# A lightning-attention block on one core: last gates ahead of the norm's root, first rows normalised by halves, two transfers moved

## The reference

```python
xn = layernorm(x)                          # x: 2048 tokens x 512, fp32
s = lightning_attn(xn, slopes, w_qkv, w_gate, w_out, norm_w)
g = silu(ffn(xn, router_w, router_b, expert_b))
x = x + s * g

# lightning_attn: 16 heads of 128, 2 sequences of 1024 tokens, blocks of 64
qkv = silu(xn @ w_qkv.T)
# per head: causal linear attention with decay exp(-slope * distance), by a state kv
out = norm_w * (out * rsqrt(mean(out * out) + 1e-6))   # mean over all 2048 values of a token
y = (sigmoid(xn @ w_gate.T) * out) @ w_out.T
# ffn: softmax over 64 router scores, the 8 largest kept;
#      flat * sum(weights) + weights @ expert_bias
```

## Time and profile before

| | us |
|---|---|
| median of 3 runs (1069.09 to 1071.27) | 1070.4 |
| the profiled execution | 1068.64 |
| its span, first to last instruction | 1066.8 |
| TensorE busy | 1047.1 (98%) |
| VectorE / ScalarE / GpSimd busy | 750.0 / 515.5 / 634.2 |

### The profile page before, as it was taken

One profiled execution on the slowest core, in us unless ns is written; L12 is line 12 of the kernel. 1 busy time (PEld: TensorE's weight loads), 2 busy tenths in 40 slices (PEclk: granted clock), 3 DMA queues, 4 the chain that ended last, 5 costly groups with the idle time before them and its releaser, 6 DMA issues.

```text
span 1066.8 us, 15997 instructions
## 1 busy us (share of the span) xinstructions
PE 1047.1 (98%) x5626; PEld 895.0 (84%) x5626; DVE 750.0 (70%) x1286; ACT 515.5 (48%) x807; POOL 634.2 (59%) x513
## 2 busy tenths in 40 slices
PE   6999999999999999999999999999999999999997
PEld 5888888888888888888878888888888888888886
DVE  6847657676765778768667766766776776876866
ACT  5746363553536335453554535435453543535344
POOL 3737475665747547474756957657474745747435
PEclk9999999999999999999999999999999999999999
DMA  7273524435252432526757264342525335242442
GB/s 243 80 276 93 140 66 130 107 99 119 58 136 65 129 89 67 140 66 172 257 191 177 94 151 129 109 110 72 135 69 130 90 104 112 51 127 82 131 127 80
DMA packets 259920, 128.12 MB, mean 120 GB/s; under 512 B 223360, under 2 KB 223488, under 8 KB 259840
## 3 DMA queue, kind: packets, MB, share of 16 engines
q1 hardware_dynamic: 259840, 127.09, 43.6%
HBM read 86.95 MB, written 40.11 MB: 119 GB/s over the span
## 4 chain that ended last, share of the span: by engine, by line
PE 92%; DVE 2%; DMA 1%; issue 1%; POOL 1%; ACT 1%; SPq 0%; POOLq 0%; DVEq 0%
PE st_ps L544 18%; PE st_ps L546 17%; PE st_ps L545 17%; PE score_ps L666 5%; PE out_ps L719 5%; PE out_ps L721 5%; PE out_ps L720 5%; PE head_ps L702 5%; PE tk_ps L685 4%; PE head_ps L705 4%; PE st_ps L532 1%; PE st_ps L534 1%; PE st_ps L533 1%; DMA xt_lo<-spill_lo 1%; POOL acc L1567 1%
## 5 line engine op out<-in xcount | busy, mean ns | idle before, releaser
L544 PE MATMUL st_ps<-xt_hi,w_hi 128*128 128x512 f32 x826 | 336.9, 408 | 1.4 <-DMA xt_lo<-spill_lo 1.3
L546 PE MATMUL st_ps<-xt_hi,w_lo 128*128 128x512 f32 x826 | 323.2, 391 | 0.0
L545 PE MATMUL st_ps<-xt_lo,w_hi 128*128 128x512 f32 x826 | 322.1, 390 | 0.0
L546 PEld LDWEIGHTS st_ps<-xt_hi,w_lo 128*128 128x128 f32 x826 | 155.0, 188 | 34.7
L1456 POOL TENSOR_TENSOR w_lo<-land_a,w_hi 128x1024 fp32r<-128x1024 f32 x44 | 107.0, 2433 | 128.7 <-ACT w_hi L1048 128.7
L544 PEld LDWEIGHTS st_ps<-xt_hi,w_hi 128*128 128x128 f32 x826 | 155.6, 188 | 31.1 <-issue 2.1
L545 PEld LDWEIGHTS st_ps<-xt_lo,w_hi 128*128 128x128 f32 x826 | 155.7, 189 | 27.9
L1436 POOL TENSOR_TENSOR w_lo<-land_a,w_hi 128x768 fp32r<-128x768 f32 x44 | 83.9, 1906 | 147.9 <-ACT w_hi L1043 147.9
L719 PE MATMUL out_ps<-wo_hi,gate_hi 128*128 128x512 f32 x240 | 96.3, 401 | 0.6 <-DVE acc L1772 0.5
L1774 DVE TENSOR_TENSOR acc<-acc,out_ps 128x512 f32<-128x512 f32 x104 | 71.3, 685 | 32.5 <-PE out_ps L721 32.2
L721 PE MATMUL out_ps<-wo_hi,gate_lo 128*128 128x512 f32 x240 | 93.8, 391 | 0.0
(11 more groups left out here) (330 smaller groups left out, 2072.9 us busy)
## 6 DMA issues: line engine op xcount, KB each, us to landing
land_a<-wgrp_dram SPq DMA_DIRECT2D x48, 512.0 KB, 3.7
v_row<-v_squares SPq DMA_DIRECT2D x120, 128.0 KB, 3.2
k_row<-k_squares SPq DMA_DIRECT2D x120, 96.0 KB, 2.9
v_squares<-v_t SPq DMA_DIRECT2D x45, 256.0 KB, 2.7
land_b<-wo_dram SPq DMA_DIRECT2D x16, 512.0 KB, 4.5
land_b<-wgrp_dram SPq DMA_DIRECT2D x14, 512.0 KB, 4.2
k_squares<-state SPq DMA_DIRECT2D x15, 384.0 KB, 2.3
k_squares<-v_t SPq DMA_DIRECT2D x15, 384.0 KB, 4.7
```

Of the source, the lines that this page charges most:

```text
L544: pe.matmul(ps[:, :], w_h2, x_h2, start=first and k == 0, stop=False, skip_group_check=True)
L545: pe.matmul(ps[:, :], w_h2, x_l2, start=False, stop=False, skip_group_check=True)
L546: end = pe.matmul(ps[:, :], w_l2, x_h2, start=False, stop=last and k == 1, skip_group_check=True)
```

## The change

The statistics of the first four tiles are combined one by one behind each tile's own. The first four tiles are normalised by halves of 256 columns: tiles 0 to 2 by VectorE, tile 3 by ScalarE, and fills 0, 1 and 2, 3 wait for their half. VectorE takes fills (0, 8) and (0, 9) before it normalises the rows of `bp` 1, and on all three engines `turn_and_score(0, 0)` (with its followers) goes ahead of `fill(1, 0)`. `swap_keys` is cut in `keys_out` and `keys_back`, and in step 7 the load of B21 goes between the two. In the tail bias products 4 to 7 and quarters 2 and 3 of the last gate block go ahead of the sums of squares; the last two squares are added on GpSimd and VectorE, not by TensorE, so a sum has one matmul call for each tile; the last gates are split on VectorE ahead of the root; tile 0's old sum goes into the output bank by a product with the identity, and its x is added by join_last; the last tile is joined and stored in halves.

```diff
@@ declarations
-        tail_square = k_t[:, 0, :]
+        tail_square = st_ps[2][:, :]
@@ SP
-            def swap_keys(ss, h):
+            def keys_out(ss, h):
...
                 sp.dma_start(k_squares, src[:, 0:2 * (NCH - 1) * HD]).then_inc(k_out, 16)
-                sp.wait_ge(k_out, 16 * (at + 1))
+
+            def keys_back(ss, h):
+                sp.wait_ge(k_out, 16 * (2 * (ss - 1) + h + 1))
                 sp.wait_ge(kv_full, unit(ss, h, 0))
...
-                swap_keys(ss, 1)
+                keys_out(ss, 1)
+                if ss == PAIRS - 1:
+                    renew_block(B21, P2)
+                keys_back(ss, 1)
...
-                if ss == PAIRS - 1:
-                    renew_block(B21, P2)
                 load_group(after, ss + 1, VAL)
...
-            for t in range(TILES):
+            for t in range(TILES - 1):
                 sp.wait_ge(summed_v, t + 1)
                 sp.dma_start(out_t[2 + t // NCH][:, t % NCH, :], acc[:, t // NCH, t % NCH, :]).then_inc(stored1, 16)
+            for i in range(2):
+                half = slice(i * (HID // 2), (i + 1) * (HID // 2))
+                sp.wait_ge(summed_v, TILES + i)
+                sp.dma_start(out_t[3][:, NCH - 1, half], acc[:, 1, NCH - 1, half]).then_inc(stored1, 16)
@@ PE, rows_there: fills 0 and 1 wait for the left halves, fills 2 and 3 for the right
+                if bp == 0 and b == 0 and c < 3:
+                    pe.wait_ge(ln_row, 3 * half + c + 1)
+                elif bp == 0 and b == 0:
+                    pe.wait_ge(ln_row_a, half + 1)
...
@@ PE, sum_squares loses the second matmul; output_rows of tile 0 start=False
-                    last = pe.matmul(ps[:, t:t + 1], acc_sq[:, tok:tok + P], ones, start=True, stop=more is None)
-                    if more is not None:
-                        last = pe.matmul(ps[:, t:t + 1], more[:, c * P:(c + 1) * P], ones, start=False, stop=True)
+                    last = pe.matmul(ps[:, t:t + 1], acc_sq[:, tok:tok + P], ones, start=True, stop=True)
@@ PE
-            fill(1, 0)
             turn_and_score(0, 0)
+            fill(1, 0)
             direct_block(5)
@@ PE, tail
             kv_products(LAST, 1, 1)
+            bias1(4)
+            bias1(5)
             direct_block(4 * FINAL + 2, range(3, 4))
             head_output(LAST, 1, 0)
-            bias1(4)
-            bias1(5)
+            bias1(6)
+            bias1(7)
             direct_block(4 * FINAL + 3, range(1))
             head_output(LAST, 1, 1, ps=score_ps)
-            direct_block(4 * FINAL + 3, range(1, 2))
-            pe.wait_ge(squared, 4 * LAST + 3)
-            pe.wait_ge(sq_added, 4 * LAST + 2)
-            sum_squares(0, tk_ps, square)
-            pe.wait_ge(squared, 4 * LAST + 4)
-            sum_squares(1, tk_ps, tail_square)
-            bias1(6)
-            bias1(7)
-            direct_block(4 * FINAL + 3, range(2, 4))
+            direct_block(4 * FINAL + 3, range(1, 4))
+            pe.wait_ge(sq_added, 4 * LAST + 3)
+            sum_squares(0, tk_ps)
+            pe.wait_ge(acted, 4 * FINAL + 3)
+            pe.matmul(tail_out[0][:, :], ident, acc[:, 0, 0, :], start=True, stop=False)
+            pe.wait_ge(last_square, 1)
+            sum_squares(1, tk_ps)
@@ ACT, head and tail
-            normalise(0, 0, 0, 2)
-            normalise(0, 0, 0, 3)
+            normalise(0, 0, 0, 3, slice(0, 256))
+            normalise(0, 0, 0, 3, slice(256, HID))
...
             act_direct(4 * FINAL + 2)
+            silu1(4)
+            silu1(5)
             act.wait_ge(head_full, 4 * LAST + 3)
             act.wait_ge(sq_added, 4 * LAST + 2)
             act.activation(square[:, :], head_ps[:, :], ACT.Square).then_inc(squared, 1)
             gate_high(LAST, 1, 0)
-            silu1(4)
+            silu1(6)
             act.wait_ge(head_full, 4 * LAST + 4)
+            act.wait_ge(gated_set, 4 * LAST + 2)
             act.activation(tail_square, score_ps[:, :], ACT.Square).then_inc(squared, 1)
-            silu1(5)
+            silu1(7)
+            act_direct(4 * FINAL + 3)
             act.preload_act_table(ACT.Sqrt)
             root_rms(4, slice(0, TILES), tk_ps)
-            act.preload_act_table(ACT.Silu)
             act.wait_ge(rms_step, 2 * RMS_STEPS)
-            scale_old(0)
-            act_direct(4 * FINAL + 3)
-            silu1(6)
-            scale_old(1)
-            tail_gate_high(1)
-            silu1(7)
-            for t in range(2, TILES):
+            for t in range(1, TILES):
                 scale_old(t)
@@ POOL, tail
             add_square(1, LAST, 0, 0)
-            for t in range(2):
+            weigh(1)
+            add_square(1, LAST, 0, 1)
+            for t in range(2, 5):
                 weigh(t)
-            add_square(1, LAST, 0, 1)
-            for t in range(2, 6):
+            add_square(1, LAST, 1, 0)
+            for t in range(5, TILES):
                 weigh(t)
-            add_x(0)
-            weigh(6)
-            add_x(1)
-            weigh(7)
-            for t in range(2, TILES):
+            for t in range(1, TILES):
                 add_x(t)
@@ DVE, row_stats (and row_roots combines only where part > 0)
+                    if part == 0:
+                        dve.wait_ge(stats_in, t + 1)
+                        dve.bn_aggr(mean_var[:, t, :], stats[:, i, :]).then_inc(ln_stat, 1)
@@ DVE
-            for c in range(2):
-                normalise(0, 0, c)
+            for c in range(3):
+                normalise(0, 0, c, slice(0, 256))
+            for c in range(3):
+                normalise(0, 0, c, slice(256, HID))
...
+            take_fill(0, 8)
+            take_fill(0, 9)
             for c in range(NCH):
                 normalise(1, 0, c)
-            for f in range(8, 12):
-                take_fill(0, f)
+            take_fill(0, 10)
+            take_fill(0, 11)
+            score_decay(0, 0, 0)
             take_fill(1, 0)
-            score_decay(0, 0, 0)
@@ DVE, tail
+            def tail_gate_high():
+                dve.wait_ge(gated_set, 4 * LAST + 4)
+                dve.tensor_copy(tail_gate_hi[:, 1, :], gated[:, 1, 1, :]).then_inc(last_high, 1)
...
-                old = acc[:, t // NCH, t % NCH, :]
+                dst = acc[:, t // NCH, t % NCH, :]
+                old = dst if t else tail_res[0]
                 dve.wait_ge(weighed_rows, t + 1)
-                dve.wait_ge(summed_p, t + 1)
-                dve.tensor_tensor(old, old, tail_out[t][:, :], ALU.add).then_inc(summed_v, 1)
+                if t:
+                    dve.wait_ge(summed_p, t)
+                for half in [slice(0, HID)] if t < TILES - 1 else [slice(0, HID // 2), slice(HID // 2, HID)]:
+                    dve.tensor_tensor(dst[:, half], old[:, half], tail_out[t][:, half], ALU.add).then_inc(summed_v, 1)
...
             states(LAST, 1, 1, 1)
+            sum1(4)
+            sum1(5)
             dve.wait_ge(squared, 4 * LAST + 3)
             gate_head(LAST, 1, 0)
-            sum1(4)
             tail_gate_low(0)
+            sum1(6)
             first_gate_low(1)
-            sum1(5)
-            rms_scale(1, slice(0, TILES), tk_ps)
-            sum1(6)
             sum1(7)
             dve.wait_ge(squared, 4 * LAST + 4)
+            dve.wait_ge(sq_added, 4 * LAST + 2)
+            dve.tensor_tensor(acc_sq[:, SEQ:2 * SEQ], acc_sq[:, SEQ:2 * SEQ], tail_square, ALU.add).then_inc(last_square, 1)
             gate_head(LAST, 1, 1, ps=score_ps)
-            weigh_last(0)
+            tail_gate_high()
             tail_gate_low(1)
-            join_last(0)
-            for t in range(1, TILES):
+            rms_scale(1, slice(0, TILES), tk_ps)
+            for t in range(TILES):
                 weigh_last(t)
                 join_last(t)
```

More of the change, by code:

```diff
@@ L387, in step @@
                         load_res(t)
-                swap_keys(ss, 0)
+                keys_out(ss, 0)
+                keys_back(ss, 0)
                 if ss == PAIRS - 1:
@@ L495, in fill @@
                 for c in range(NCH):
-                    if f // 2 in (B11, B12) and f % 2 == 0:
-                        rows_there(bp, b, c)
+                    if f // 2 in (B11, B12) and f % 2 == 0 or (bp, f) == (0, 2):
+                        rows_there(bp, b, c, k // 2)
                     rows = acc[:, b, c, :] if f >= 8 else row_tile(bp, b, c)
@@ L500, in fill, with rows_there @@
                 last.then_inc(xt_turned, 1)
-            def rows_there(bp, b, c):
-                if bp == 0 and c < 2:
-                    pe.wait_ge(ln_row, 2 * b + c + 1)
+            def rows_there(bp, b, c, half):
+                if bp == 0 and b == 0 and c < 3:
+                    pe.wait_ge(ln_row, 3 * half + c + 1)
+                elif bp == 0 and b == 0:
+                    pe.wait_ge(ln_row_a, half + 1)
+                elif bp == 0 and c < 2:
+                    pe.wait_ge(ln_row, 6 + c + 1)
                 elif bp == 0:
-                    pe.wait_ge(ln_row_a, 2 * b + c - 1)
```

(23 more changed lines are left out.)

29 lines of the change are left out of this document (15 added, 14 removed).

## The result

The changed kernel took 1062.58 us (median of 5, 1061.60 to 1063.13), the kernel before 1070.84 beside it (median of 5, 1069.09 to 1071.33): ratio 0.9924, 95% interval 0.9909 to 0.9938. The sign and the likeliest case were right. The profiled execution took 1062.85 us with a span of 1061.1. Against the profile before that is 5.79 less, almost exactly the sum of 5.76, though not by exact terms: as the last part shows, errors of up to 0.6 us in the single terms cancel, which is luck. Against the medians it is 8.3 less. So the question for the runs is where the other 2.5 us come from: 2.2 by which the profiled execution before lay under its median of 1070.84, and 0.3 by which the one after lies over its own.

The account below looks back on a forecast made before the run. The prediction took TensorE, busy 98% of the span, as the bound outside its gaps, and VectorE at the end. Terms 0.45 + 1.27 + 1.1 + 2.94 = 5.76 us off the median 1070.4 gave 1064.6, range 1063.0 to 1067.4.

Parts of the forecast that it names:

- sign: Whole kernel: the change makes it faster, chance 0.88; same 0.06, slower 0.06.
- likeliest case: Whole kernel: all four gains reach the end, median 1064.6 us, chance 0.64.
- the step that moved the sum onto the median: Whole kernel: gains taken off the profiled execution, to 1062.9 us, were moved onto the median, 1070.4 - 5.8 = 1064.6.
- tail term: Kernel's end: last join 2.64 us earlier and last store 0.3 shorter, 2.94 in all, bounds 2.2 and 3.6.
- Head: Kernel's start: statistics combined one by one and normalising by halves start TensorE's fills earlier, 0.45 us, bounds 0.2 and 0.7.
- Fills: Around 37 us: fill(0, 10) finds its bank free and TensorE's wait goes, 1.27 us, bounds 0.8 and 1.4.
- Reload: Steps 7 and 8: B21 loaded ahead of keys_back shortens TensorE's waits for token blocks, 1.1 us, upper bound 1.25.
- the cover of 2.7: Step 8: keys may come 2.7 us late before TensorE waits for ScalarE's result; 1.5 us of lateness was taken.
- the 4.1: Reload: the most the keys could come late behind B21's 1 MB, 4.1 us; ring order was said to favour this end.
- GpSimd binds: Tail rival: GpSimd's add_x at 1.75 us each puts the last join 2.35 us behind forecast, 1067.0 us, chance 0.11.
- early gains are lost: Rival: head and fills gains don't reach the end as another input comes at its own time, 1066.3 us, chance 0.13.
- The keys' rival: Reload: keys served only with the burst of reloads behind them make the kernel slower, 1075.3 us if landing at 532, chance 0.06.

Follow-up runs that it names:

- half_sums: Kernel before without the eight one-column calls for the last heads' squares, wide bias products issued three times in their place: 1068.27 us, ratio 0.9989.
- no_reload: Changed kernel with the B21 load put back behind keys_back: 1063.57 us, ratio 0.9945 to the kernel before.
- no_tail: Changed kernel with the old tail, all edits behind the last step undone: 1067.22 us, ratio 0.9973 to the kernel before.
- only_tail: Kernel before with the tail's edits alone; head, fills and reload as before: 1065.18 us, ratio 0.9956.
- before_again: Kernel before, nothing edited, run and profiled once more: 1070.29 us, beside 1070.17 for the kernel before.
- after_sums_long: Changed kernel with the identity product ahead of the sums and each one-column call issued twice, 3.5 us in a row: 1066.44 us.
- after_sums_apart: Changed kernel with each one-column call issued twice, the identity product left between the two halves: 1066.00 us.
- sums_split: Kernel before with sum_squares(0) issued a quarter of a direct block earlier, dividing the one-column calls in two stretches: 1069.34 us, ratio 0.9993.
- root_earlier: Changed kernel with the identity product behind sum_squares(1) and sum1(7) ahead of first_gate_low(1) on VectorE: 1063.16 us, ratio 0.9940.

## Where the prediction was right, and where it failed

**What failed is the step that moved the sum onto the median.** "The profiled execution would take 1062.9; the median 1070.4 - 5.8 = 1064.6" takes a profile of 1068.64 and a median of 1070.4 for the same kernel with a constant between them. The 1.8 us between them were mostly not a constant: in that execution the clock stayed at 1.00 until TensorE was done (the windows above), while 59 of 75 executions have a mean clock of 0.997 or less, which among the profiles only those with a fall in the tail have. The tail term should have held it: I priced the eight calls that go at their own 1.74 us, and they also take the fall with them, which half_sums puts at 1.8 us of the median (1.2 by its ratio, 0.1 to 2.1). With 1.8 the sum is 7.6 and the time 1062.8. The rest of the 8.3 is mostly the draw: the five executions beside the result have a median 0.7 over that of the 75. The three timed executions that I had, 1069.09 to 1071.27, all lay above the profiled one; that was the place to ask what differs between executions. The Trainium skill, "TensorE: Matmul & The Clock Gate", Part 1, describes a watcher of TensorE's activity in free-running windows and calls its effect run-variable. The Trainium skill says the second of the slow matmuls at a kernel's start. The runs show the like in the tail: the clock of the same kernel falls in one execution and not in another. I used that rule for the head, where it would have moved the term by 0.2, and not here.

**Head: forecast 0.45, found 0.33** at 26 us (matmuls of the two profiles compared one by one), within the bounds. The halves came 0.34 apart and not 0.30, and the last row tile landed 0.2 later. The first full-speed matmul moved by 0.38, the second fill by 0.24. The clock column of the windows can't show this rise, as it reads 1.00 from the start in both profiles; the durations do (0.78, 0.63 and 0.60 against 0.40 before). By the free-running rule the rise might have stood still; here it didn't, though TensorE's start itself lay between 9.1 and 10.4 us in the profiles, by the landing of the first rows, so that one pair doesn't settle it.

**Fills: 1.27, found 1.64** (the shift goes from 0.33 to 1.97 between 26 and 40 us). The mechanism and the cover by the scores were right. The term was too small because I took the bracket for the loss. It counts from the modelled end of the matmul before, 0.39 behind its start; from start to start the step from that matmul to fill(0, 10) took 1.66 and takes 0.23 now, 1.43 less. The other 0.2 are the fills themselves, whose own banks came late too: 0.59 and 0.50 apart before, 0.43 and 0.44 now.

**Reload: 1.1, found 0.5** in the pair of profiles. Over all profiles the waits for token blocks sum to 1.25, 1.31, 0.78, 0.78, 1.41 and 0.73 without the edit (mean 1.04), and to 0.58, 0.17, 0.82, 0.83, 0, 0.81, 0.40 and 0.23 with it (0.48): 0.56. What failed is "everything behind it on SP is issued about 1 us earlier". The keys' four issues stretch from 2.67 us to 5.02 behind B21 (3.58 to 5.02 in the eight profiles with the edit, 2.67 in all six without), and the value weights are issued at 518.02, where no_reload, at the same progress, has 516.64. The gain that is left is, as I read it, B21's bytes moved while the queues were idle: in the two microseconds from 512 the queues move 152 and 385 GB/s, and 0 and 105 in no_reload. The keys come 2.0 us later than in no_reload (519.99 against 517.97) and not 1.5, inside the cover of 2.7, but not by much: ScalarE's instruction behind them ends at 523.05, 0.5 ahead of the matmul that needs it (523.58). The Trainium skill, "DMA: Bandwidth & Descriptors", Queues, rings and completion order, has descriptors consumed in ring order. The direction agrees; the 4.1 that I tied to it did not come.

**Tail, in the profiles: 2.94, found 2.8.** The old end less the new is 5.65 at the last join (1064.34 to 1058.69), of which 2.89 had been there on entry: 2.76 by VectorE, forecast 2.64. The smaller last store, forecast 0.3, gave 0.05: the span ends 2.41 behind the last join instead of 2.46. The identity product took 0.94 (forecast 0.89), the sums 0.81 twice from start to start (0.87), the cast 0.43 (0.7), and VectorE bound from weigh_last(0) to the last join. That GpSimd binds or that early gains are lost didn't happen: of 1.97 us at 40 us none was given back. The keys' rival, a slower kernel, didn't happen either. Some 0.4 us more came in small steps between the four places, which no edit accounts for.

In the medians the tail is worth 4.6 (no_tail) or 4.8 (only_tail): 2.8 and, as the difference, about 1.9 of clock. What stays open: why the fall comes in some executions and not in others, and why it lasts 3 us in two profiles and nearly 7 in the other two. It was also not tried whether one-column calls placed much earlier than the tail would be harmless.

## What to carry to other kernels

A forecast from one profile holds for that execution; where the timed runs spread by more than the forecast's terms, look at a second profile of the same kernel, above all its granted clock, before moving a difference onto the median. Here 3.5 us of one-column fp32 matmul calls, in which TensorE counted as busy, could bring its clock down, so they cost more than their duration; where operands can be added on another engine first, as here the squares, that is worth a try. A transfer moved ahead on a queue can also slow the issue of what is behind it, here from 2.67 us to as much as 5.02.

## What the runs showed of the hardware

- The granted clock fell from 1.00 to 0.50 with TensorE 100% busy, in profiles of four kernels, each with 3.5 us of one-column fp32 calls close together (before_again, no_tail, after_sums_long, after_sums_apart). In the profiles of eight kernels with 1.75 us of them it stayed at 1.00 until TensorE's last matmul. The profiles of before and sums_split, with 3.5 us, stayed there too, so it is a matter of the execution. By mean clock, 59 of 75 executions of the kernel before lie at 0.997 or less; none of the 11 of half_sums is under 0.998, and none of the 37 of the seven kernels with the new tail and no doubled sums is under 0.999.
- Four issues of the same DMAs took SP 2.67 us in the six profiles with free queues and 3.58 to 5.02 in the eight behind 1 MB of others.
- VectorE's cast of the last gates from SBUF to SBUF (128x512, fp32 to fp32r) took 0.43 us in eight profiles with the new tail and 0.69 in root_earlier. In the changed kernel it starts at 1045.19, as GpSimd's last weigh ends (1045.22); in root_earlier at 1044.42, 0.40 ahead of that end (1044.82). GpSimd's work beside it is the likely cause, which no run tested.
